# A flamingo block with routed experts: clears spread over the tiles, second normalisation on ScalarE, another beginning

## The reference, cut to what matters

```
x = x + tanh(g_xattn[0]) * xattn(layernorm(x), ctx, ctx)      # 16 heads of 16, softmax over 256 keys
x = x + tanh(g_ffn[0]) * ffn(layernorm(x))

ffn:  scores = softmax(xf @ w_router)                          # 8 experts
      w, idx = top_k(scores, 2)
      moe    = sum over the two of w * (silu(xf @ w1[e]) * (xf @ w3[e])) @ w2[e]
      shared = (silu(xf @ ws1) * (xf @ ws3)) @ ws2             # hidden 512 both times
      out    = shared / 3 + moe * 2 / 3
```

## Time and profile before

| | us |
|---|---|
| median of three runs | 816.92 |
| the profiled execution, its own time | 814.12 |
| its span, first to last instruction | 812.4 |
| TensorE busy | 769.9 (95%) |
| TensorE's weight loads busy | 686.5 (85%) |
| VectorE busy | 538.8 (66%) |
| POOL busy | 430.7 (53%) |
| ScalarE busy | 413.4 (51%) |

### The profile page before, as it was taken

The page is one execution under the profiler, slowest core; times in us unless marked ns, Lnnn a source line. Parts: engine busy times, 40 slices in busy tenths (PEclk is TensorE's granted clock), DMA queues, the critical chain, the costliest instruction groups (busy, mean ns, idle before and its releaser), DMA issues.

```text
span 812.4 us, 19406 instructions
## 1 busy us (share of the span) xinstructions
PE 769.9 (95%) x6955; PEld 686.5 (85%) x6956; DVE 538.8 (66%) x1118; ACT 413.4 (51%) x690; POOL 430.7 (53%) x489
## 2 busy tenths in 40 slices
PE   4888999999999998898997999999999999999998
PEld 3756777777777776578997999999999999999998
DVE  5677889998888888857644444444444444446897
ACT  5667777777777767653324333333334334333332
POOL 5633446666666654457772476656756675236000
PEclk9999999999999999999998999999999999999999
DMA  6854557776666654244394354444543422317622
GB/s 213 272 179 158 173 185 231 234 235 209 210 209 209 198 182 145 93 170 138 110 248 113 96 155 130 117 114 131 142 116 78 111 70 58 72 53 306 233 93 79
DMA packets 129150, 127.34 MB, mean 157 GB/s; under 512 B 55232, under 2 KB 111040, under 8 KB 129088
## 3 DMA queue, kind: packets, MB, share of 16 engines
q1 hardware_dynamic: 114896, 80.34, 33.4%
q0 software_dynamic: 14192, 46.19, 16.9%
HBM read 75.32 MB, written 50.91 MB: 155 GB/s over the span
## 4 chain that ended last, share of the span: by engine, by line
PE 61%; POOL 10%; DMA 9%; issue 7%; DVE 7%; ACT 4%; SPq 2%; POOLq 1%; ACTq 0%; DVEq 0%
PE bank L562 7%; PE bank L563 6%; PE bank L564 6%; PE bank L643 6%; PE bank_ss L614 6%; PE bank_sm L627 4%; POOL w_l L1635 4%; DMA y_d<-y_s,y_rows 3%; PE bank_sm L562 3%; PE bank_ss L562 3%; PE bank_sm L563 3%; PE bank_sm L564 3%; PE bank_ss L564 3%; PE bank_ss L563 3%; PE bank L650 3%
## 5 line engine op out<-in xcount | busy, mean ns | idle before, releaser
L1248 DVE TENSOR_REDUCE row_max<-bank_sm 128x4 f32<-128x1024 f32 x124 | 151.5, 1222 | 37.8 <-PE bank_sm L627 36.2
L953 ACT ACTIVATE probs_T<-bank_ss 128x1024 f32<-128x1024 f32 x123 | 126.5, 1028 | 18.9 <-PE bank_ss L614 17.9
L1227 DVE TENSOR_TENSOR gT_l<-gg,gT_h 128x1024 fp32r<-128x1024 f32 x49 | 66.8, 1363 | 102.0 <-ACT gT_h L1084 100.1
L562 PE MATMUL bank_sm<-xg_h,w_h 128*128 128x256 f32 x400 | 114.3, 286 | 7.1 <-DVE xg_l L1227 7.1
L562 PE MATMUL bank_ss<-xg_h,w_h 128*128 128x256 f32 x400 | 113.2, 283 | 0.5 <-DVE gg L1434 0.5
L563 PE MATMUL bank_sm<-xg_h,w_l 128*128 128x256 f32 x400 | 113.6, 284 | 0.0
L564 PE MATMUL bank_sm<-xg_l,w_h 128*128 128x256 f32 x400 | 113.5, 284 | 0.0
L564 PE MATMUL bank_ss<-xg_l,w_h 128*128 128x256 f32 x400 | 112.9, 282 | 0.0
L563 PE MATMUL bank_ss<-xg_h,w_l 128*128 128x256 f32 x400 | 112.9, 282 | 0.0
L562 PE MATMUL bank<-w_h,gT_h 128*128 128x256 f32 x392 | 111.1, 284 | 1.5 <-DVE gT_l L1227 1.5
L563 PE MATMUL bank<-w_h,gT_l 128*128 128x256 f32 x392 | 110.9, 283 | 0.0
(11 more groups left out here) (204 smaller groups left out, 1945.6 us busy)
## 6 DMA issues: line engine op xcount, KB each, us to landing
qk_d<-qk_s SPq DMA_DIRECT2D x64, 256.0 KB, 2.8
w_raw<-wall POOLq DMA_DIRECT2D x27, 512.0 KB
k<-qk_d SPq DMA_DIRECT2D x48, 256.0 KB
q<-qk_d SPq DMA_DIRECT2D x48, 256.0 KB
xq<-xs_d SPq DMA_DIRECT2D x140, 64.0 KB
y_pairs<-y_d POOLq DMA_DIRECT2D x16, 512.0 KB, 9.7
x<-x SPq DMA_DIRECT2D x16, 256.0 KB, 4.7
c_s<-ctxT SPq DMA_DIRECT2D x16, 256.0 KB, 3.1
```

The costliest lines, as they stand in the source:

```text
L562: pe.matmul(out, ah, bh, start=first and k == 0, stop=False)
L953: act.activation(pT[:, 2 * (pv % 4):2 * (pv % 4) + 2, :].rearrange("p h t -> p (h t)"), exp_bank(V.b, pv)[:, :], ACT.Exp, scale=D ** -0.5) ...
L1227: return v.tensor_tensor(dst, ps, high.bitcast(F32), ALU.subtract)
L1248: v.tensor_reduce(mx[B.slot][:, :, :].rearrange("p t (r q) -> p r t q", r=2)[:, :, :, p], max_bank(B.b, p)[:, :].rearrange("p (r t k) -> p ...
```

## The change

- *Clears.* POOL's four clears and their semaphore go. SP clears list 0, then 1 and 2, then, in a loop that is unrolled for u = 1 to 10, one list more behind `load_rows(u)` of u = 1, 3, 5, 7 and 9, with a wait for the earlier ones every second tile.
- *Second normalisation.* For batches 0 to 12 ScalarE does it as scale * x + bias (rstd and -mean * rstd), behind its exp of slot 7. VectorE negates the mean, POOL makes the root ahead of its second half of `xn_s` and multiplies for the bias. TensorE turns the result in slot 0 of the next iteration, behind `turn_max`.
- *End of the attention.* VectorE takes variance and norm of batch 14 ahead of the places of batch 13; POOL cuts part 0 ahead of the root, and scatters after it.
- *Beginning.* 4 keep-warm matmuls in place of 14, and none behind; the bias product of the output goes to another bank and one iteration earlier; the maxima of batch 0 are turned, copied and sent in two halves (heads in another order in `mx`); SP sends the q terms of batch 0 ahead of the half-out of k of batch 1, and the half-outs of batch 2 ahead of its terms; POOL makes the low half of q of batch 0 ahead of its second half of `xn_s`; v of the fourth slot is cleared one iteration later.

```diff
+HALF = PAIRS // 2
+        first_mT = (mT[0:2 * HALF, :], oT_h[0:2 * HALF, 0, :])
+        def by_scalar(batch):
+            return batch.b < NB - 3
@@ SP
             def max_rows(C):
-                sp.wait_ge(mT_ok, C.n(1, 1))
+                sp.wait_ge(mT_ok, C.n(1, 2))
...
-                    ... mT[8 * par:8 * par + 8, :].bitcast(F32)).then_inc(mrow, 16)
+                    ... mT[par:H:2, :].bitcast(F32)).then_inc(mrow, 16)
+            def first_rows(half):
+                sp.wait_ge(mT_ok, half + 1)
+                for par in range(2):
+                    row = ROWS * par + MROW
+                    sp.dma_start(q4[0][row:row + 1, HALF * half:HALF * half + HALF, :].bitcast(F32),
+                                 first_mT[half][par:2 * HALF:2, :].bitcast(F32)).then_inc((first_mrow, mrow)[half], 16)
...
             load_x(Batch(3))
+            terms_in(b0, 0)
             half_out(b1, 1)
-            terms_in(b0, 0)
             load_c(Batch(3))
+            terms_in(b1, 1)
             half_out(b1, 0)
-            terms_in(b1, 1)
             load_x(Batch(4))
             terms_in(b1, 0)
+            first_rows(0)
             half_out(b2, 1)
+            half_out(b2, 0)
+            first_rows(1)
             terms_in(b2, 1)
-            half_out(b2, 0)
-            max_rows(b0)
             terms_in(b2, 0)
...
-            clear_behind(sp, (2, 4, 6), z_done)
+            clear_behind(sp, (1, 2), z_done)
...
-            sp.wait_ge(z_done, 16 * 3)
-            sp.wait_ge(z_pool, 16 * 4)
+            sp.wait_ge(z_done, 16 * 2)
...
-            with sp.Fori(1, last3) as u:
+            for u in range(1, 2 * NX - 5):
+                if u % 2 and u > 1:
+                    sp.wait_ge(z_done, 16 * ((u + 3) // 2))
+                load_routed(u + 3)
+                load_rows(u)
+                if u % 2 and (u + 5) // 2 < NX:
+                    clear_behind(sp, ((u + 5) // 2,), z_done)
+            sp.wait_ge(z_done, 16 * (NX - 1))
+            with sp.Fori(2 * NX - 5, last3) as u:
                 load_routed(u + 3)
                 load_rows(u)
@@ TensorE
             def scores_to_exp(V, pv):
-                if pv == 0:
+                if pv == 0 and V.b == 0:
+                    pe.wait_ge(first_mrow, 32)
+                if pv == (0 if V.b else HALF):
                     pe.wait_ge(mrow, V.n(32, 32))
...
             def scores_to_max(B, p):
-                moved(pe, mx_ok, B.n(PAIRS, p - among_first(B, 1)))
+                moved(pe, mx_ok, B.n(PAIRS, p - (among_first(B, 1) or B.b == 1 and p == 0)))
+                if among_first(B, 1) and p == 1:
+                    pe.wait_ge(gbo_ok, 1)
...
+            def turn_first(half):
+                pe.wait_ge(mx_ok, HALF * half + HALF)
+                moved(pe, mT_ok, half)
+                for qc in range(TC):
+                    r = pe.transpose(T0[0:2 * HALF, qc * P:(qc + 1) * P], mx[0][:, qc, 2 * HALF * half:2 * HALF * (half + 1)], ident)
+                r.then_inc(mT_ps, 1)
...
                     if B and among_first(B, 1) and p == 0:
-                        keep_warm(SS[:, 0:512], 14)
-                    if B and B.b == 1 and p == 1:
                         keep_warm(SS[:, 0:512], 4)
+                    if B and among_first(B, 1) and p == HALF + 1:
+                        pe.wait_ge(xnTl_ok, A.n(1, 1))
+                        turn_first(0)
                     if B:
                         scores_to_max(B, p)
+                    if p == 0 and C and among_first(C, 1):
+                        turn_first(1)
                     if p == 0 and C and not among_first(C, 1):
                         turn_max(C, S2)
+                    if p == 0 and S3 and by_scalar(S3):
+                        turn_norm(S3)
...
-                    if p == 7 and A and A.b == 1:
+                    if p == 7 and A and A.b == 0:
...
-                            r = pe.matmul(T0[:, 0:E], bv_s[:, k, :], ...)
+                            r = pe.matmul(SS[:, 512:512 + E], bv_s[:, k, :], ...)
...
-                        turn_norm(S2)
-                if B and among_first(B, 1):
-                    pe.wait_ge(mx_ok, PAIRS - 1)
-                    keep_warm(SM[:, 0:512], 4)
-                    turn_max(B, None)
+                        if not by_scalar(S2):
+                            turn_norm(S2)
@@ ScalarE
+            def first_max(half):
+                act.wait_ge(mT_ps, half + 1)
+                act.activation(first_mT[half], T0[0:2 * HALF, 0:L], ACT.Copy, scale=-1.0).then_inc(mT_ok, 1)
+            def norm(S2):
+                act.wait_ge(shift2_ok, S2.n(1, 1))
+                moved(act, sc_done[1], S2.n(32, 32 - R * 32))
+                for t in range(TC):
+                    r = act.activation(xn2_s[S2.slot][:, t, 0:E], x2_s[:, t, :], ACT.Identity, bias=shift2[:, t:t + 1], scale=rstd2[:, t:t + 1])
+                r.then_inc(xn2_ok, 1)
...
+                    if p == 7 and S2 and by_scalar(S2):
+                        norm(S2)
@@ VectorE
             def add_eps(mv, done):
                 settle()
+                if mv is bmv2:
+                    v.tensor_scalar(mean2[:, :], mv[:, :, 0], -1.0, None, ALU.mult)
...
-                    if p == 7 and S2:
+                    if p == 7 and S2 and not by_scalar(S2):
                         norm(S2)
...
-                if A and A.b == R - 1:
+                if A and A.b == R:
                     clear_v(R)
...
             residual_stats(x14)
+            residual_variance(x14)
+            norm(x14)
             positions(x13, rk_tail)
-            residual_variance(x14)
             list_slots(x13)
             divide(x15)
-            norm(x14)
@@ POOL
+                def norm_terms():
+                    root(bmv2, rstd2, var2_ok, S2, rstd2_ok)
+                    if by_scalar(S2):
+                        po.wait_ge(rstd2_ok, S2.n(1, 1))
+                        po.tensor_tensor(shift2[:, :], mean2[:, :], rstd2[:, :], ALU.mult).then_inc(shift2_ok, 1)
...
                     po.tensor_tensor(xn_s[:, :, :], x_s[Eb.x_slot][:, :, :], bmv..., ALU.subtract).then_inc(xc_ok, 1)
+                    if A and among_first(A, 1):
+                        leave_low(0, qh_ok, ql_ok)
+                    if S2:
+                        norm_terms()
...
-                if S2:
-                    root(bmv2, rstd2, var2_ok, S2, rstd2_ok)
-                if A:
+                if S2 and not Eb:
+                    norm_terms()
+                if A and not among_first(A, 1):
                     leave_low(0, qh_ok, ql_ok)
...
-            scatter(Batch(NB - 4), 1)
...
+            cut(1, 0, which=(0,))
             root(bmv2, rstd2, var2_ok, x14, rstd2_ok)
-            cut(1, 0, which=(0,))
+            scatter(Batch(NB - 4), 1)
...
-            clear_behind(po, (1, 3, 5, 7), z_pool)
```

More of the change, by code:

```diff
@@ L197, in build @@
             rstd2 = sb(a, "rstd2", [P, TC])
+            mean2 = sb(a, "minus_mean2", [P, TC])
+            shift2 = sb(a, "shift2", [P, TC])
             pT = sb(a, "probs_T", [P, 8, TC * L])
@@ L409, in max_rows @@
             def max_rows(C):
-                sp.wait_ge(mT_ok, C.n(1, 1))
+                sp.wait_ge(mT_ok, C.n(1, 2))
                 for par in range(2):
                     row = ROWS * par + MROW
-                    sp.dma_start(q4[C.slot][row:row + 1, :, :].bitcast(F32), mT[8 * par:8 * par + 8, :].bitcast(F32)).then_inc(mrow, 16)
+                    sp.dma_start(q4[C.slot][row:row + 1, :, :].bitcast(F32), mT[par:H:2, :].bitcast(F32)).then_inc(mrow, 16)
+            def first_rows(half):
[4 more added lines that the diff above has]
+                                 first_mT[half][par:2 * HALF:2, :].bitcast(F32)).then_inc((first_mrow, mrow)[half], 16)
             def one(i):
@@ L751, in one @@
                         if C:
-                            pe.wait_ge(mT_ok, C.n(1, 1))
+                            pe.wait_ge(mT_ok, C.n(1, 2))
                         if S2:
@@ L813, in one @@
                         for k in range(EC):
-                            r = pe.matmul(T0[:, 0:E], bv_s[:, k, :], wt_raw[:, 3, k * E:(k + 1) * E], start=k == 0, stop=k == EC - 1)
+                            r = pe.matmul(SS[:, 512:512 + E], bv_s[:, k, :], wt_raw[:, 3, k * E:(k + 1) * E], start=k == 0, stop=k == EC - 1)
                         r.then_inc(bo_ps, 1)
@@ L979, in one @@
             def one(i):
-                Eb, A, F, C, S, S3 = (stage(i, k) for k in (4, 3, 2, 0, -1, -3))
+                Eb, A, F, C, S, S2, S3 = (stage(i, k) for k in (4, 3, 2, 0, -1, -2, -3))
                 def q_or_k(side, bnk, ps, half):
@@ L1004, in before @@
                                        ACT.Copy).then_inc(vr_ok, 1)
-                    if p == 0 and C:
-                        act.wait_ge(mT_ps, C.n(1, 1))
+                    if p == 0 and C and among_first(C, 1):
+                        first_max(1)
+                    if p == 0 and C and not among_first(C, 1):
```

(10 more changed lines are left out.)

13 lines of the change are left out of this document (4 added, 9 removed).

## The result

The changed kernel took **804.72 us** (median of 4 runs, 802.83 to 805.95), the kernel before 816.95 beside it: ratio 0.9845, 95% interval 0.9821 to 0.987: faster, by more than the 0.5% that the prediction called no change. Forecast were 798.6 in a range of 792 to 809. The gain is 12.2 us where 18.3 were forecast. The profiled execution took 805.26 (span 803.4; of before 812.4).

A forecast was written before the change was run, and what follows sets the result against it. TensorE, busy 95% of the span, was taken as the bound, so only its idle or half-clock time could be won. 7.8 + 6.8 + 1.7 + 2.0 = 18.3 us off 814.1 gave 795.8, plus 2.8 to the median: 798.6, range 792 to 809.

The forecast's parts named there:

- Edit 1: Clears where the routed tiles begin: most moved behind tile 7's rows, closing TensorE's hole; 7.8 us, bounds 0 and 7.8.
- I take all 7.8: Transition to routed tiles: 70 missing matmuls at 9 per us are all won back once tile 7's rows land in time.
- I take 0 for all five: Routed tiles: the five clears left in SP's queue, lists 3 to 7, cost TensorE nothing.
- rival (d): Routed tiles: clears in SP's queue delay the scatter chain, total 824.1, 3%; milder, 1 us each, 803.6, 7%.
- Edit 2: Second normalisation in the attention iterations, moved to ScalarE with a later turn: 6.8 us, bounds 2 and 8.
- 1.0 for the first, 0.7 for each of the others: Three slow iterations: us gained as the root precedes the weight load and the norm leaves VectorE; together 2.4 us.
- 12 times: Iterations of batches 3 to 14: a TensorE gap of 0.37 us closes in each, 4.4 us together.
- rival (b): Iterations: ScalarE's norm delays v and minus_max, TensorE still waits for exp; gain 2.4 instead of 6.8, total 803; 12%.
- Edit 3: End of the attention: TensorE's gaps for norm of batch 14 and xg_l shrink; 1.7 us of 2.1.
- Edit 4: Beginning: earlier q terms and fewer keep-warm matmuls bring the first scores sooner; net 2.0 us, bounds -2 and 4.
- rival (a): Beginning: fewer fillers let TensorE drop to its lower clock once or twice more; about -3 there, total 803.5; 20%.
- I keep the same dip and no second one: Beginning: TensorE's clock falls once ahead of the first scores, as in the kernel before, and not again.

The follow-up runs named there:

- the doubled clears: Changed kernel with a second write of 514 KB, to another buffer, behind each of the five clears among the routed tiles; one run, 803.7 us.
- the swap: Changed kernel with SP's half-out of q of batch 1 put ahead of the k terms of batch 1; 801.65 us, ratio 0.9841.
- the 14 fillers: Changed kernel with 14 filler matmuls ahead of the first scores again instead of 4; 805.32 us, ratio 0.9883.
- the second median: Changed kernel measured once more, unchanged, beside the later variants on the same chip; 798.01 us, ratio 0.9816.
- The mends: Changed kernel with q's half-out of batch 1 ahead of its k terms, and batches 11 and 12 normalised on VectorE; both together 796.51 us, ratio 0.9798.
- NB - 5: Changed kernel with batches 11 and 12 normalised by VectorE again and turned in slot 7; 799.28 us, ratio 0.9815.

## Why the prediction was right or wrong

**Edit 1 (forecast 7.8): the mechanism was right, the size was that of one profile.** The step that missed is "I take all 7.8". It counted missing matmuls in a single execution in which the wait was 10.19 us and the clock was low in two windows; four others show 5.5 to 6.3, and a stretch shorter by 3.1 to 3.6. The clears ahead were worth 4.7, less 0.5 for the five in the loop, 4.2 (5.3 alone, between medians). Since the sum was then set against a median by adding 2.8, the error went straight into the forecast. "I take 0 for all five" was nearly right (0.5, not clear of the spread). How far off rival (d) was, the doubled clears don't tell. "Each costs SP about 1 us of issue" was too much: the five rows of SP's queue show 0.41 to 0.42.

**Edit 2 (forecast 6.8): right in the ten iterations, wrong behind them.** By the windows 204.7 became 198.6, 6.0 us, where the same steps gave 10 x 0.37 + 2.4 = 6.1. Inside it the split was wrong: "1.0 for the first, 0.7 for each of the others" was put down to POOL's load ahead of the root; the early root gave half of that, and the rest came with the norm's leaving VectorE, where it takes 1.7 to 1.9 us in those iterations with the early root and without. In the last iterations "12 times" failed for batches 11 and 12. TensorE was idle for 2.0 to 2.5 us of each there anyway (17.84 less 15.80, 17.62 less 15.17), so the late turn closes no gap, and ScalarE comes late with its two activations: this is rival (b), in that place alone, which I had not asked for. What it costs depends on the clock: from nothing to 5 us (49.1 to 54.9 with ScalarE's norm, 48.4 to 49.9 with VectorE's).

**Edit 3 (forecast 1.7): right.** From the 14th to the 16th `logits` 31.9 became 30.5 in the mean, 1.4 us. No wait of TensorE for norm or xg_l stands there. But "I estimate the root 2 us earlier" gives only part of the reason. Against the 14th `logits` the root came 1.2 us earlier in this pair (7.5 us behind it instead of 8.7), and VectorE waits for it longer. The larger part is the norm of batch 14 itself, first before, then changed:

```profile
364.08 2.45 DVE L1314 TENSOR_SCALAR xn<-x_s,bn_mv,rstd 128x256 f32<-128x256 f32 x2 [0.50 <-POOL rstd L1653]
```

```profile
362.49 0.74 DVE L1368 TENSOR_SCALAR xn<-x_s,bn_mv,rstd 128x256 f32<-128x256 f32 x2 [2.84 <-POOL rstd L1707]
```

Before, POOL's cut of part 0 ran beside it (from 363.99 on); now the cut is over when the norm starts. The prediction had no term for that.

**Edit 4 (forecast +2.0): rival (a) holds, in a mild form.** The mean start is 100.8 with the old beginning (five profiles) and 100.4 with the new one (six, without the swap and the 14 fillers), so it gave about 0.5, less than the spread of either (99.9 to 101.6 and 99.4 to 102.0); alone it lost 1.5 between medians, with an interval that just leaves out no change. The first scores came 1.9 us sooner, as forecast. Two steps failed. "The new order delays the half-outs of batch 2" looked one batch too far: the half-out of q of batch 1 was held first, by SP's wait for k's landing. And "I keep the same dip and no second one": the clock of 18 to 60 us is 0.92 to 0.96 with the old beginning and 0.80 to 0.88 with the new one, without exception. A clock lower by 0.04 over these 42 us is 3.4 us more at the lower level and 1.7 lost; the new beginning has one to four such stretches more. What takes the clock down there is not shown: the fillers ahead of the scores are not it, the swap took 0.6 to 2.2 us from a wait for DMA and the clock stayed at 0.88, and the eight fillers behind the scores were not tried alone. The Trainium skill (TensorE: Matmul & The Clock Gate, HAM oscillation) says that short bursts between waits for DMA bring the half rate back. The direction of these rows agrees (0.88 against 0.96); that the waits are the cause, they don't show. I had given the rival 20%.

**The sum.** 4.2 + 6.0 + 1.4 + 0.5 is 12.1 where 18.3 were forecast: 3.6 of the missing 6.2 are edit 1, 1.5 edit 4, 0.8 edit 2. Off it go 0 to 5 in the last iterations; measured were 12.2 and, again, 14.5. So the stages explain the gain only as far as the spread of the clock lets them, and that 804.72 lies well inside the range owes something to a kernel before that ran at 816.95 beside it and at 812.5 to 815.2 in the three later comparisons. That the second median (798.01) lies on my 798.6 is no merit of the sum: the kernel before took 812.5 beside it and not 816.9.

**The clock, over all runs.** The 35 runs of the kernel before that come with these experiments go from 808.8 to 817.3, with a mean clock of 0.998 to 0.987; a line through them gives 6.0 us for 0.01 of clock. The changed kernel's first four runs had 0.983 to 0.987, the second four 0.991 to 0.996: 0.008 in the mean, 4.8 of the 6.7 us between them. Put to 0.992 by that line, the means are 813.5 before, 800.7 and 798.9 after. In the same way the clears alone come to 3.8 less than before, the normalisation alone to 6.0, the beginning alone to 0.8 less: with 1.4 for the end 12.0, against 12.8 and 14.6 for all together. The single runs scatter about the line by 1.4 us, so this is an estimate; it says that the lower clock took most of what the normalisation alone and the beginning alone did not give. Why the same code got a lower clock the first time (the chip, or the moment) stays open.

**The mends.** NB - 5 has the old times in three stretches and has not shown a long fall of the clock in two profiles; the changed kernel has one profile with and one without. SP's swap takes 0.6 to 2.2 us from a wait of TensorE (1.19 in both of its profiles against 1.8 to 3.4), but the starts with it, 98.4 and 99.8, overlap with those without. Together they beat the kernel before by 2.0%; against the changed kernel on the same chip the 1.5 us is inside the spread, so that they beat it too is not shown.

## What to carry to other kernels

A wait that ends on a crowded DMA queue has another size in each execution. Before its price goes into a sum, read it in a second profile, and compare the sum with the execution that it was read from before you move it to the median. Where a gain is counted per iteration, look at the iterations with less work separately: what fills a gap in one is a new link in the chain of the other. Ahead of a wait for a landing in a shared issue queue, look at the very next instruction in that queue, and not at the batch after it.

## What the runs showed of the hardware that was not expected

The granted clock fell in stretches of 3.4, 6.8 or about 10 us, and not at the same places for the same instructions: in the beginning of the clears-only kernel for 6.8 us near 48.5, in that of before, with the same instructions, for 3.4 us near 32. One stretch of 3.4 us costs up to 1.7 us or 0.2%, and the runs of the kernel before differ by 8.5 us. The Trainium skill (TensorE: Matmul & The Clock Gate, Part 1: The HAM clock gate) says that the slow matmuls at the start vary from run to run; here the same holds in the middle of a kernel, with 3.4 us in one run of the last iterations and 10.4 in another. And VectorE's norm of 128x256, twice, took 0.73 us in one iteration and 1.70 to 1.92 in another with the same shapes, and 2.45 for batch 14: each time POOL instructions of 1.0 to 1.3 us ran beside it, and with these moved away from batch 14 it took 0.74.
